# Filter and projection stage: an opening written out for each engine, weights loaded without a staging buffer, filter parameters computed in groups of 32 steps

## The reference

```python
dtA = A * dt[:, None]                      # 192 positions x 64 states, A complex
C = C * (jnp.exp(dtA) - 1.0) / A           # C: the input x, complex
K = 2.0 * jnp.einsum('chn,hnl->chl', C, jnp.exp(dtA[:, :, None] * ell)).real
h = K
h = h + attn(layernorm(h))                 # q, k, v, g = x @ Wq, Wk, Wv, Wg; rope; decayed causal scores; gate; @ Wo
h = h + ffn(layernorm(h))                  # top-1 gated heads, softmax attention with shared k and v
```

## Time and profile before

| | |
|---|---|
| median of three runs | 1316.46 us |
| the profiled execution | 1319.74 us |
| its span in the trace | 1318.0 us |
| PE busy | 1227.0 us, 93% |
| VectorE busy | 723.5 us, 55% |
| ScalarE busy | 559.1 us, 42% |
| GpSimd busy | 518.9 us, 39% |
| first matmul | 43.59 us |

### The profile page before, as it was taken

How to read it: one execution, slowest core, us unless ns; L and a number is a source line. 1 busy time by engine, 2 the same in 40 slices (tenths; PEclk the granted TensorE clock), 3 DMA queues, 4 the chain that set the end, 5 groups by cost and what they waited for, 6 DMA issues and landing times. The chain is left out here.

```text
span 1318.0 us, 22927 instructions
## 1 busy us (share of the span) xinstructions
PE 1227.0 (93%) x8280; PEld 1016.7 (77%) x8280; DVE 723.5 (55%) x1360; ACT 559.1 (42%) x1769; POOL 518.9 (39%) x722
## 2 busy tenths in 40 slices
PE   0389999999999999699999999989999999999997
PEld 0368888888888888577877887878888788887875
DVE  7686655666666532455555445435464554645544
ACT  3344333444433321434343332224555555454546
POOL 2757666766676641333333233120321213122121
PEclk9999999999999999999999999889899999999999
DMA  4132222222222225966656535153252706436061
GB/s 155 66 119 96 105 103 114 95 104 105 102 112 91 112 88 190 313 186 209 211 173 176 153 116 145 48 120 82 48 110 52 161 15 148 89 74 137 6 133 34
DMA packets 63359, 154.78 MB, mean 117 GB/s; under 512 B 9616, under 2 KB 26128, under 8 KB 61712
## 3 DMA queue, kind: packets, MB, share of 16 engines
q1 hardware_dynamic: 63248, 153.33, 39.7%
HBM read 67.19 MB, written 56.62 MB: 94 GB/s over the span
## 5 line engine op out<-in xcount | busy, mean ns | idle before, releaser
L1682 ACT ACTIVATE probs<-psum,row_max 128x128 f32<-128x128 f32 (+1 forms) x384 | 142.9, 388 | 48.6 <-DVE row_max L1848 36.7
L1848 DVE TENSOR_REDUCE row_max<-psum 128x2 f32<-128x384 f32 (+1 forms) x128 | 79.2, 619 | 82.4 <-PE psum L2079 43.8
L1010 ACT ACTIVATE square_scratch<-psum 128x128 f32<-128x128 f32 x192 | 50.7, 274 | 172.8 <-PE psum L1243 172.8
L1979 POOL TENSOR_TENSOR h_rows<-h_rows,y_normed 128x512 f32<-128x512 f32 x24 | 30.7, 1281 | 228.2 <-DVE y_normed L1865 228.2
L1956 POOL TENSOR_TENSOR picked_rows<-picked_rows 128x768 f32<-128x768 f32 (+1 forms) x64 | 61.1, 954 | 104.3 <-DVE picked_rows L1830 100.6
L1183 POOL TENSOR_TENSOR rr<-ss,consts_r 128x3 f32<-128x3 f32 x64 | 13.2, 206 | 195.8 <-ACT square_scratch L1010 192.7
L712 PE MATMUL psum<-m,basis 128*128 128x64 f32 x384 | 48.9, 284 | 43.6 <-POOL basis L664 43.6
L1856 DVE COPY raw_f<-psum 128x512 f32<-128x512 f32 x64 | 44.2, 691 | 80.4 <-PE psum L2092 80.3
L683 POOL TENSOR_TENSOR stage<-stage 128x512 f32<-128x512 f32 x48 | 81.6, 1718 | 14.5 <-DVE stage L565 14.5
L712 PEld LDWEIGHTS psum<-m,basis 128*128 128x128 f32 x384 | 49.6, 203 | 45.7 <-issue 43.6
L1682 ACT ACTIVATION_READ_ACCUMULATOR probs<-psum,row_max 128x1 f32 x384 | 80.5, 210 | 0.0
(11 more groups left out here) (269 smaller groups left out, 3594.6 us busy)
## 6 DMA issues: line engine op xcount, KB each, us to landing
qk<-stage SPq DMA_DIRECT2D x24, 512.0 KB, 2.6
v<-stage SPq DMA_DIRECT2D x24, 512.0 KB, 2.6
g<-gate_rows SPq DMA_DIRECT2D x24, 512.0 KB, 2.8
qk_rows<-qk SPq DMA_DIRECT2D x16, 512.0 KB, 7.3
q_stack_even<-q_t_high SPq DMA_DIRECT2D x32, 224.0 KB, 5.5
q_stack_even<-q_t_low SPq DMA_DIRECT2D x32, 224.0 KB, 6.7
q_stack_odd<-q_t_high SPq DMA_DIRECT2D x32, 224.0 KB, 5.4
q_stack_odd<-q_t_low SPq DMA_DIRECT2D x32, 224.0 KB, 6.7
```

What stands on the lines that cost most here:

```text
L1010: last = nc.scalar.activation(sqs[:, h % 2, t], psum[:, OB[h % 2], t * RV:(t + 1) * RV], ACT.Square, accum_out=ss[:, h % 2, t:t + 1])
L1682: last = nc.scalar.activation(pr[:, g % 2, c], psum[:, SB[g % 3], c], ACT.Exp, bias=mx[:, g % 3, x:x + 1], accum_out=dsum[:, t, h:h + 1])
L1848: V.reduce_max(mx[:, g % 3, 0:nh], psum[:, SB[g % 3], 0:nh * w].rearrange("p (h n) -> p h n", h=nh), AX, negate=True).then_inc(s_max.sem, 1)
L1979: G.tensor_tensor(h, h, yn[:, (NT * i + t) % 2].rearrange("p h f -> p (h f)"), ALU.add).then_inc(added.sem, 1)
```

## The change

Slots begin at 1 in place of -4. What came before is written out in a function `first` for each engine, in a new order: ScalarE takes the first sines ahead of all weight copies; VectorE takes the corners of chunk 0 and the basis sums of units 0 and 1, which GpSimd did, and the weight splits are spread between its other work; unit 2's spectrum moves on PE from behind WK of unit 0 to behind its first WG. Chunk 2 (units 4 and 5) is made in slot 1 in place of slot 0, and `build` of unit 4 moves from slot 1 to slot 2, behind `gates` of unit 1.

The raw weights have a place of their own: each lies where its low part will be, and the split writes over it. `load_w` waits for nothing; all six are issued at the start, between the other loads.

The factors are computed in six groups of 32 positions, 24 steps each, some on both components at once: `group(0)` in the opening, `group(1)` in slot 1 between `reduce` of chunk 2 and `x_split`, groups 2 to 5 in slots 4, 8, 12 and 16 between `build` and `scale`. `g4` holds two groups; `corners` waits for its group. In the diff below the four functions `first` are those of ScalarE, VectorE, GpSimd and PE, in this order.

```diff
-    w_pairs = [(sb(n + "_high", [P, KC, D], F32R), sb(n + "_low", [P, KC, D], F32R)) for n in names]
-    w_hi, w_lo = [hi for hi, _ in w_pairs], [lo for _, lo in w_pairs]
+    w_hi, w_lo, w_raw = [], [], []
+    for n in names:
+        w_hi.append(sb(n + "_high", [P, KC, D], F32R))
+        with ExitStack() as under:
+            w_raw.append(under.enter_context(nc.sbuf_tensor(n + "_raw", [P, KC, D], F32)))
+        w_lo.append(sb(n + "_low", [P, KC, D], F32R))
...
-    tmp = basis_mem[:, 0:20 * T].rearrange("p (n t) -> p n t", n=20)
+    angle_tmp = basis_mem[:, 0:6 * T].rearrange("p (n t) -> p n t", n=6)
+    halves = sb("half_tan_sin_cos", [P, 3, T])
+    group_tmp = sb("group_tmp", [P, 8, 2, GC])
...
-    g4 = sb("g4", [P, 4, T])
+    g4 = sb("g4", [P, 2, 4, GC])
...
+    GROUP_AT, GROUP_STEPS = 8, 24
...
+    def corners(eng, E, c):
+        q = c[1] % 2
+        co, si = cs[:, q, :, NB0 + NB1:NL], sn[:, q, :, NB0 + NB1:NL]
+        eng.wait_ge(scaled.sem, chunk_at(scaled, c, 1))
+        n, hs = c[1] // 2, slice(q * HCH, (q + 1) * HCH)
+        eng.wait_ge(par_dve, GROUP_AT + GROUP_STEPS * (n + 1))
+        g = lambda k: bcast(g4[:, n % 2, k, hs], 2, NA)
+        E.tensor_tensor(xyt[:, 0], g(0), co, ALU.mult)
+        E.tensor_tensor(xyt[:, 1], g(1), si, ALU.mult)
+        E.tensor_tensor(xyt[:, 2], g(2), si, ALU.mult)
+        E.tensor_tensor(xyt[:, 3], g(3), co, ALU.mult).then_inc(xy_chain.sem, 1)
+        eng.wait_ge(xy_chain.sem, chunk_at(xy_chain, c, 1))
+        E.tensor_tensor(xy[:, q, 0], xyt[:, 0], xyt[:, 1], ALU.add)
+        E.tensor_tensor(xy[:, q, 1], xyt[:, 2], xyt[:, 3], ALU.add).then_inc(xy_ready.sem, 1)
...
-            if n >= 2:
-
-                sp.wait_ge(w_high, n - 1)
-                sp.wait_ge(w_low, n - 1)
-            sp.dma_start(raw[:, n % 2], d["w_r"][n]).then_inc(w_in[n % 2], 16)
+            sp.dma_start(w_raw[n][:, :, :], d["w_r"][n]).then_inc(w_in[n], 16)
...
         load_w(0)
+        load_c((0, 0))
         load_w(1)
-        load_c((0, 0))
+        sp.dma_start(ident[:, :], d["ident"]).then_inc(const_in, 16)
         load_c((0, 1))
-        sp.dma_start(ident[:, :], d["ident"]).then_inc(const_in, 16)
+        load_w(2)
+        load_w(3)
         sp.dma_start(rope_t[:, :, :].rearrange("p u f -> p (u f)"), d["rope"]).then_inc(const_in, 16)
-        for n in range(2, NP):
-            load_w(n)
+        load_w(4)
+        load_w(5)
 
         def store(name, u, src, s):
             sp.dma_start(d[name][bass.ds(u[0] * UNITS + u[1], 1)].rearrange("o p f -> (o p) f"), src).then_inc(s.sem, 16)
...
                 k_evac(step_of(u, 2))
             if valid(u):
                 v_evac(u, 0)
+            if u == (0, 1):
+                trigonometry((0, 2))
+            if valid(u):
...
+        def first():
+            trigonometry((0, 0))
+            w_copy(0)
+            digits((0, 0))
+            for n in range(1, NP):
+                w_copy(n)
+            k_evac((0, 0))
+            angle_size((0, 1))
+            h_evac((0, 0))
+            sines((0, 1))
+            norm((0, 0))
+            x_split((0, 0))
+            decay_exp((0, 1))
+            k_evac((0, 1))
+            digits((0, 1))
+            h_evac((0, 1))
+            norm((0, 1))
+            v_evac((0, 0), 0)
+            v_evac((0, 0), 1)
+            x_split((0, 1))
+            g_tanh((0, 0), 0)
+            k_evac((0, 2))
+
+        first()
+        slots(slot, 1)
...
+        def group(k):
+            cols = slice(k * GC, (k + 1) * GC)
+            ar, ai, b0, b1 = a[:, cols], aim[:, cols], br[:, cols], bi[:, cols]
+            th, s, c = tn[:, cols], sh[:, cols], ch[:, cols]
+            x = lambda j: group_tmp[:, j, 0]
+            y = lambda j: group_tmp[:, j, 1]
+            both = lambda j: group_tmp[:, j]
+            out = g4[:, k % 2]
+            if k >= 2:
+                dve.wait_ge(xy_ready.sem, chunk_at(xy_ready, (0, 2 * k - 3), 1))
+            step(V.tensor_tensor(x(0), ar, ar, ALU.mult))
+            step(V.tensor_tensor(y(0), ai, ai, ALU.mult))
+            step(V.tensor_tensor(x(1), x(0), y(0), ALU.add))
+            step(V.reciprocal(y(1), x(1)))
+            step(V.tensor_scalar(x(0), y(1), 2.0, None, ALU.mult))
+
+            if k == 0:
+                dve.wait_ge(par_act, 2)
+            step(V.tensor_scalar(x(1), th, -1.0, 1.0, ALU.mult, ALU.add))
+            step(V.reciprocal(y(1), x(1)))
+            step(V.scalar_tensor_tensor(x(2), th, 2.0, y(1), ALU.mult, ALU.mult))
+
+            if k == 0:
+                dve.wait_ge(par_act, 4)
+            step(V.scalar_tensor_tensor(x(3), s, -2.0, s, ALU.mult, ALU.mult))
+            step(V.scalar_tensor_tensor(y(3), s, 2.0, c, ALU.mult, ALU.mult))
+
+            step(V.scalar_tensor_tensor(y(2), x(3), 1.0, x(2), ALU.add, ALU.mult))
+            step(V.tensor_tensor(x(4), y(2), x(3), ALU.add))
+            step(V.scalar_tensor_tensor(y(4), x(2), 1.0, y(3), ALU.add, ALU.mult))
+
+            step(V.tensor_tensor(both(5), both(4), bcast(b0, 1, 2), ALU.mult))
+            step(V.tensor_tensor(both(6), both(4), bcast(b1, 1, 2), ALU.mult))
+            step(V.tensor_tensor(x(7), x(5), y(6), ALU.subtract))
+            step(V.tensor_tensor(y(7), y(5), x(6), ALU.add))
+
+            step(V.tensor_tensor(both(5), both(7), bcast(ar, 1, 2), ALU.mult))
+            step(V.tensor_tensor(both(6), both(7), bcast(ai, 1, 2), ALU.mult))
+            step(V.tensor_tensor(x(4), x(5), y(6), ALU.subtract))
+            step(V.tensor_tensor(y(4), x(6), y(5), ALU.add))
+            step(V.tensor_tensor(out[:, 2:4], both(4), bcast(x(0), 1, 2), ALU.mult))
+
+            step(V.tensor_scalar(out[:, 0], out[:, 2], sign, -1.0, ALU.mult, ALU.mult))
+            step(V.tensor_scalar(out[:, 1], out[:, 3], sign, None, ALU.mult))
+            assert n[0] == GROUP_AT + GROUP_STEPS * (k + 1)
...
+            if u == (0, 2):
+                build((0, 4))
+            if even(u) and valid(step_of(u, 4)):
                 reduce(chunk(step_of(u, 4)))
...
+            if u == (0, 1):
+                reduce((0, 2))
+                group(1)
+            elif valid(step_of(u, 3)):
                 build(step_of(u, 3))
...
+            if u[1] % 4 == 0 and valid(step_of(u, 4)):
+                group(u[1] // 4 + 1)
             if even(u) and valid(step_of(u, 4)):
                 scale(chunk(step_of(u, 4)))
...
-            if valid(step_of(u, 1)) and u[1] >= 0:
+            if valid(step_of(u, 1)):
                 x_split(step_of(u, 1))
+            if u == (0, 1):
+                scale((0, 2))
             if valid(u):
...
+        def first():
+            group(0)
+            scale((0, 0))
+            corners(dve, V, (0, 0))
+            build((0, 0))
+            basis_add(dve, V, (0, 0))
+            reduce((0, 1))
+            build((0, 1))
+            row_stats((0, 0))
+            dve.wait_ge(rstd.sem, rstd.of((0, 0), 1))
+            basis_add(dve, V, (0, 1))
+            split_weights(0)
+            x_split((0, 0))
+            split_weights(1)
+            scale((0, 1))
+            split_weights(2)
+            split_weights(3)
+            dve.wait_ge(const_in, 32)
+            rope((0, 0), 0)
+            row_stats((0, 1))
+            build((0, 2))
+            split_weights(4)
+            rope((0, 0), 1)
+            split_weights(5)
+            x_split((0, 1))
+            build((0, 3))
+            gates((0, 0), 0)
+
+        first()
+        slots(slot, 1)
...
+        def first():
+            decay((0, 0))
+            moving((0, 0))
+            decay((0, 1))
+            moving((0, 1))
+            scales((0, 0))
+            moving((0, 2))
+            scales((0, 1))
+            basis_add(pool, G, (0, 2))
+            rope_add((0, 0), 0)
+            rope_add((0, 0), 1)
+            moving((0, 3))
+            basis_add(pool, G, (0, 3))
+            decay((0, 2))
+
+        first()
+        slots(slot, 1)
...
+        def first():
+            u, nxt = (0, 0), (0, 1)
+            spectrum(u)
+            row_transposes(u)
+            x_transposes(u)
+            spectrum(nxt)
+            pe.wait_ge(x_low.sem, x_low.of(u, 1))
+            project(u, WQ, 0).then_inc(qk_sum.sem, 1)
+            row_transposes(nxt)
+            project(u, WK, 1).then_inc(qk_sum.sem, 1)
+            project(u, WV, 2).then_inc(v_sum.sem, 1)
+            project(u, WV + 1, 3).then_inc(v_sum.sem, 1)
+            x_transposes(nxt)
+            pe.wait_ge(roped.sem, roped.of(u, 1))
+            project(u, WG, 4).then_inc(g_sum.sem, 1)
+            spectrum((0, 2))
+            pe.wait_ge(roped.sem, roped.of(u, 2))
+            project(u, WG + 1, 5).then_inc(g_sum.sem, 1)
+
+        first()
+        slots(slot, 1)
```

More of the change, by code:

```diff
@@ L175, in stage_p @@
     const_in = sem("const_in_p")
-    w_in = [sem(f"w_in{q}") for q in range(2)]
+    w_in = [sem(f"w_in{n}") for n in range(NP)]
     w_high = sem("w_high")
@@ L247, in even, with slots, basis_add @@
```

(47 more changed lines are left out.)

109 lines of the change are left out of this document (10 added, 99 removed).

## The result

The changed kernel takes 1337.64 us, median of four runs (1334.72 to 1338.87), against 1315.94 us of the kernel before in the same rounds: slower. The ratio on record is 1.0144, with a 95% interval of 1.0119 to 1.0169; the quotient of these two medians is 1.0165, near the upper end of it. The profiled execution took 1338.87 us with a span of 1337.1; before it was 1319.74 and 1318.0, so 19.1 us more. The forecast was 1336, from a sum of +19.6.

A forecast was written before the change was run, and what follows sets the result against it. TensorE, full in the unit loop, was taken as the bound, so its waits count in full. -10.0 (opening) + 29.6 (groups) = +19.6: 1339.3 profiled, median 1336; own range 1326 to 1347, 8 in 10 from 1312 to 1348.

The forecast's parts named there:

- The opening: Ahead of unit 3: 24 narrow steps start scale 7.6 us sooner; 10.0 us gained by unit 3, bounds 5 and 15.
- the wait before the spectrum of unit 4: PE in unit 2: the basis of unit 4 comes late, a wait of 5.0 us and 1.6 for the clock.
- the 0.9 said for x_split of unit 3: Between units 2 and 3: x_split of unit 3 is late next, 0.9 us more.
- seven megabytes at 400 GB/s: Opening: loads in front of the last weight need about 25 us; the weights are not in the chain.
- The groups in the loop: Slots 4, 8, 12, 16: group delays x_low 8.1 us, PE waits 5.8 plus 1.6 for clock; 29.6 us lost.
- 0.88 of GpSimd's own time: VectorE beside GpSimd: VectorE loses 0.88 of GpSimd's time alone; 5.1 us for a slot's mt, m and basis sum.
- A: Slots 4 to 16 and reduce of chunk 1: VectorE keeps the port, GpSimd waits; 1302 to 1309 us, chance 0.15.
- B: Group slots: half of GpSimd's operations pass during reciprocals and waits, PE waits near 3 us; 1314 to 1322, chance 0.17.
- C: Opening gain lost to waits at units 1 and 4, each PE wait doubled by low clock; 1352 us, chance 0.10.
- D: Opening: scale might wait for exp instead of group(0); 0.5 us, counted with the forecast, no chance of its own.

The follow-up runs named there:

- the second experiment: The changed kernel with GpSimd waiting, in slots 4, 8, 12 and 16, for the group's end before moving of unit u+3; 1315.52 us, ratio 0.9976.
- odd-slot kernel: The changed kernel with groups 2 to 5 one slot earlier, in slots 3, 7, 11 and 15, between build and x_split; 1326.53 us, ratio 1.0058.

## Why the prediction was right

**What bounds.** The forecast had PE without a gap in the loop, so that each wait counts in full, and the table adds up. With the groups moved behind the split, the loop has no wait behind unit 4 and its pace is the old one, 19.14 us a unit.

**The opening.** Said: scale at 18.5, first spectrum 27.9, WQ 46.1, unit 1 at 73.7, unit 2 at 93.2, unit 3 at 119.9, 10.0 brought. Measured: 18.64, 27.37, 43.89, 70.90, 90.34, 118.54, 11.3. VectorE's two ends of the parameter steps (compare):

```profile
12.64 0.19 DVE L551 TENSOR_TENSOR group_tmp<-params 128x32 f32<-128x32 f32 x1
12.87 0.19 DVE L552 TENSOR_TENSOR group_tmp<-params 128x32 f32<-128x32 f32 x1
...
18.64 0.62 DVE L529 TENSOR_TENSOR sin_cos<-sin_cos,mag 128x448 f32<-128x448 f32 x1
```

A step costs 0.225 us from start to start (0.24 was taken), a reciprocal 0.39. Two misses cancel in part, and that is luck. From the first spectrum to WQ of unit 0 I had 18.2 us and it was 16.5; half of the difference is reduce of chunk 1 beside GpSimd, which ended at 34.22 (said 35.6, from a start 0.5 later). From unit 2 to unit 3 I had 26.7 and it was 28.2: the wait before the spectrum of unit 4 was 4.84 (said 5.0), but the lower clock behind it cost 4.2, not 1.6, for it covered the spectrum (3.67 in place of 1.89) and WV behind it; the 0.9 said for x_split of unit 3 did not come. One sum of the prediction does not follow: seven megabytes at 400 GB/s take 18 us, not 25. Nothing in the forecast hangs on it, and in the trace the loads at the start move at 330 to 450 GB/s until 24 us.

ScalarE, opening (compare):

```profile
14.34 1.28 ACT L370 ACT_TABLE_LOAD   x1
15.64 0.58 ACT L370 ACTIVATE mag<-mag 128x448 f32<-128x448 f32 x1
```

exp ends at 16.22, as said, and the first activation starts as soon as the table is there. The Trainium skill (ScalarE: Activation LUTs, What ACT_TABLE_LOAD costs) adds a drain to each switch; by an estimate with its figure exp would have ended near 19.0. The trace does not agree.

**The groups in the loop.** Said: x_low 12.8 us behind build's end, a wait of 5.8, 1.6 for the clock, 29.6 in all. Measured: 12.0, a delay of 5.3 to 5.6, 1.5 to 2.8 for the clock (2.3 in the mean), 30.7. Two terms were mis-sized and cancel: the group beside GpSimd came out too long by 0.7 (next paragraph), the clock too short by 0.7; WQ alone took 1.5 to 2.4 us longer than its 2.86. The mechanism is shown by the second experiment: the same place, GpSimd held off, and 5.95 us of steps.

**How the two engines share.** I took 0.88 of GpSimd's own time as lost, whatever its operations. That share came from a miscount. Beside reduce of chunk 1 stood six GpSimd operations and not five; the sixth was another mt, and the last step of reduce (45.28, 1.13 in place of 0.39) was held beside it (trace of the kernel before):

```profile
44.73 1.43 POOL L652 TENSOR_TENSOR mt<-cin,xy 128x512 f32<-128x512 f32 x1
```

With its 1.05 the loss of 5.89 us falls on 7.75 of GpSimd, a share of 0.76. At 0.76 the four operations of a slot (5.8 us alone) cost 4.4 in place of 5.1, and x_low comes 12.1 behind build's end with a wait of 5.1. That is what slot 8 shows: the steps lost 4.4 (10.36 from the first to scale, 6.00 in the opening), x_low came at 12.0, and PE waited 4.98. That the price follows the long operations only was not in the prediction either; here it made no difference, as all four GpSimd operations are long, but it spoilt my expectation for the odd slots.

The Trainium skill (SBUF — State Buffer, Who interferes with whom) says that a VectorE instruction contends with GpSimd when it has two SBUF inputs or runs in a two-port mode, `tensor_scalar` among those that can, and otherwise not. The rows of slot 8 agree in kind: the two long `TENSOR_SCALAR` steps have one input and were held (0.77, 2.32), and the reciprocal, one input too, took its 0.35 at 236.72 in the middle of m (236.49 to 237.84).

**The sum.** It came out at +19.4 for +19.6, closer than its parts, which were off by 1.3 (the opening) and 1.1 (the groups) in opposite directions. The mechanism was right; the last microsecond is luck. The bounds given for the parts add up to 1326 to 1345, not to the 1347 that stands there.

**The rivals.** A (VectorE keeps the port) falls: four steps are held in every group. A time in its range, 1302 to 1309, came once the groups stood behind the split, for another reason. B (half of GpSimd's operations pass, waits near 3) falls by the waits of 5, though its remark on reciprocals was right. C falls: the opening held. D did not occur: exp ended at 16.2, scale began behind the group.

## What to carry to other kernels

A chain of many short VectorE steps costs little where nobody waits for its end, and its full length plus most of every long GpSimd operation beside it (here 6.0 us and 4.4) where an instruction that feeds TensorE stands behind it: put it behind that instruction, not ahead of it. Before VectorE's spare time is spent, ask what GpSimd does in that stretch, and count all of its operations. And price a TensorE wait by its length: in these profiles waits of 1.4 to 1.6 us cost themselves, and behind 11 of the 13 of 2.0 us and more the lower clock came on top.

## What the runs showed of the hardware

**TensorE's clock after a wait in the loop.** WQ has 12 matmuls and takes 2.86 us at 2.4 GHz. The table has the waits before WQ, of all profiles, ahead of which PE had been busy without a gap for over 25 us.

| wait, us | cases | WQ took, us |
|---|---|---|
| 1.43 to 1.58 | 5 | 2.86 to 2.90, full clock in all |
| 2.00 to 2.16 | 4 | 2.85, 2.86, 4.12, 4.44 |
| 3.34 | 1 | 4.18 |
| 3.67 | 4 | 5.28, 4.47, 4.46, 4.45 |
| 4.98 to 5.26 | 4 | 5.29, 4.35, 5.15, 5.29 |

The clock can fall after PE has resumed. PE's timeline in the odd-slot kernel:

```profile
224.59 0.50 PE L820 MATMUL psum<-wq_high,x_high 128*128 128x512 f32 x1 [3.67 <-DVE x_low L613]
224.93 0.40 PE L820 MATMUL psum<-wq_low,x_high 128*128 128x512 f32 x1
...
225.68 0.63 PE L820 MATMUL psum<-wq_low,x_high 128*128 128x512 f32 x1
```

PE resumed at 2.4 GHz and dropped to 1.2 about 1 us later; behind the waits of 5 us, the one of 3.34 and one of the four of 3.67 it was low from the first matmul. Equal waits had different outcomes, so the length alone doesn't decide it; what else does stays open.

**VectorE's small steps.** 128x32 takes 0.19 us and 128x192 0.36; 128x32 reciprocals 0.35 and 128x192 ones 1.35. Six times the columns cost 2.0 times the time over the 24 steps (12.1 against 6.0), so cutting a chain of waiting steps into six groups makes VectorE's total three times as long.
